# Another order of the calls on TensorE, ScalarE and VectorE in the recurrent part of a gated delta-rule kernel

## The reference, cut to what matters

```python
mixed = silu(conv4(xn @ W_qkv))            # 4 taps per channel, over time
q, k, v = split(mixed)                     # 16 key heads, each used by 2 value heads
q, k = l2norm(q) * DK ** -0.5, l2norm(k)
def step(S, xs):                           # token by token, S is 128 x 128 for a head
    S = S * exp(g_t)
    S = S + beta_t * k_t[:, None] * (v_t - k_t @ S)[None, :]
    return S, q_t @ S
o = o * rsqrt(mean(o * o) + 1e-6) * norm_w * silu(xn @ W_z)
s = o @ W_out
```

## Time and profile before

| what | value |
|---|---|
| median of 3 runs | 2795.55 us (2793.66 to 2805.6) |
| the profiled execution's own time | 2802.01 us |
| its span in the profile | 2800.1 us |
| TensorE busy | 2619.4 us, 94% |
| DVE, ScalarE, GpSimd busy | 71%, 58%, 38% |
| mean granted TensorE clock | 0.985 |

### The profile page before, as it was taken

How to read it: one execution, slowest core, us unless ns; L and a number is a source line. 1 busy time by engine, 2 the same in 40 slices (tenths; PEclk the granted TensorE clock), 3 DMA queues, 4 the chain that set the end, 5 groups by cost and what they waited for, 6 DMA issues and landing times.

```text
span 2800.1 us, 87430 instructions
## 1 busy us (share of the span) xinstructions
PE 2619.4 (94%) x34330; PEld 1946.0 (69%) x34330; DVE 2001.6 (71%) x4880; ACT 1610.8 (58%) x5046; POOL 1075.5 (38%) x1391
## 2 busy tenths in 40 slices
PE   2999997999999999999999999999999999999995
PEld 2456655777777777777777777777777777777774
DVE  5322235888878887888778877887778878888773
ACT  2111114666666666666666666666666666666662
POOL 0312203444444444444444444444444444444440
PEclk8999998999999999999999999999999999999997
DMA  4322301111111111111111111111111111111112
GB/s 148 76 53 64 64 1 53 46 54 46 53 46 54 46 54 46 54 46 54 46 53 46 54 46 53 47 43 49 43 49 50 49 49 50 50 50 50 50 50 64
DMA packets 225654, 146.99 MB, mean 52 GB/s; under 512 B 187456, under 2 KB 195936, under 8 KB 225120
## 3 DMA queue, kind: packets, MB, share of 16 engines
q1 hardware_dynamic: 219104, 123.58, 15.5%
q0 software_dynamic: 6144, 17.83, 2.8%
HBM read 115.81 MB, written 2.70 MB: 42 GB/s over the span
## 4 chain that ended last, share of the span: by engine, by line
PE 66%; DVE 8%; ACT 3%; issue 2%; DMA 2%; SPq 1%; POOL 1%; DVEq 0%; POOLq 0%; ACTq 0%
PE rps L809 12%; PE rps L734 8%; PE rps L742 8%; DVE conv L1262 6%; PE rps L696 4%; PE rps L826 4%; PE rps L713 4%; PE rps L865 3%; PE rps L856 3%; PE rps L839 3%; PE rps L680 3%; PE rps L706 3%; PE rps L774 3%; PE rps L783 3%; PE rps L683 2%
## 5 line engine op out<-in xcount | busy, mean ns | idle before, releaser
L1262 DVE SCALAR_TENSOR_TENSOR conv<-rps,w_in,conv 128x509 f32<-128x509 f32 (+2 forms) x768 | 572.0, 745 | 64.6 <-ACT conv L1050 46.4
L809 PE MATMUL rps<-xnT,w_in 128*128 128x512 f32 x1024 | 504.3, 615 | 13.9 <-DVE cols L1244 13.0
L1461 POOL TENSOR_TENSOR decay_b<-decay,beta_k 128x512 f32<-128x512 f32 x128 | 130.6, 1042 | 487.6 <-DVE beta_k L1278 487.6
L1412 POOL TENSOR_TENSOR o_t<-o_sq,q_mean 128x8 f32<-128x8 f32 x65 | 13.4, 206 | 691.0 <-ACT gated L983 691.0
L809 PEld LDWEIGHTS rps<-xnT,w_in 128*128 128x128 f32 x1024 | 174.8, 190 | 148.2 <-issue 125.2
L742 PE MATMUL rps<-w_z,xnT 128*128 128x256 f32 x1040 | 275.1, 387 | 1.0 <-ACT z L999 0.7
L1050 ACT ACTIVATE conv<-rps,w_in 128x512 f32<-128x512 f32 x256 | 176.1, 688 | 164.5 <-PE rps L809 161.5
L734 PE MATMUL rps<-w_outn,gatedT 128*128 128x256 f32 x1056 | 241.3, 381 | 1.0 <-ACT gatedT L993 0.7
L734 PEld LDWEIGHTS rps<-w_outn,gatedT 128*128 128x128 f32 x1056 | 201.6, 191 | 49.7 <-issue 23.8
L1064 ACT ACTIVATE qkT<-conv 128x512 f32<-128x512 f32 x128 | 80.5, 629 | 222.1 <-DVE conv L1262 222.1
L742 PEld LDWEIGHTS rps<-w_z,xnT 128*128 128x128 f32 x1040 | 183.1, 191 | 21.6 <-ACT z L999 1.1
(11 more groups left out here) (217 smaller groups left out, 6477.4 us busy)
## 6 DMA issues: line engine op xcount, KB each, us to landing
sums_row<-g_rows SPq DMA_DIRECT2D x65, 1024.0 KB, 5.0
scale<-comb_rows POOLq DMA_DIRECT2D x40, 256.0 KB, 5.0
w_in<-in_w_in SPq DMA_DIRECT2D x17, 520.0 KB, 3.5
bq<-bmat SPq DMA_DIRECT2D x256, 32.0 KB, 2.0
inv<-xq SPq DMA_DIRECT2D x256, 32.0 KB, 1.9
w_z<-in_w_z SPq DMA_DIRECT2D x17, 256.0 KB, 2.6
w_out<-in_w_out SPq DMA_DIRECT2D x17, 256.0 KB, 5.0
invT<-xqT SPq DMA_DIRECT2D x128, 32.0 KB, 2.2
```

What stands on the lines that cost most here:

```text
L809: last = nc.tensor.matmul(ps[PROJ_BANK[j]][:, :], w_in[:, m * 4 * P + j * P:m * 4 * P + (j + 1) * P], xnT[:, m, b * T:(b + 1) * T], start= ...
L1262: nc.vector.scalar_tensor_tensor(conv[:, j, shift:T], ps[PROJ_BANK[j]][:, 0:T - shift], w_in[:, k:k + 1], conv[:, j, shift:T], ALU.mult, A ...
L1461: nc.gpsimd.tensor_tensor(decay_b[:, us, :], decay[:, us, :], beta_k2[:, us].unsqueeze(2).to_broadcast([P, NC_, C]), ALU.mult).then_inc(db ...
```

## The change

The same calls stand in another order in the lists of TensorE, ScalarE and DVE, inside the loop over steps. GpSimd's and SyncE's lists are as before. No call is added or dropped, and the waits inside a call go with it.

```diff
@@ TensorE
                     project(0)
+                    halves_w(n)
                     by_token(1)
-                    halves_w(n)
                     project(2)
...
                     solve(0)
                     project(3)
-                    attend(0)
                     pe.wait_ge(tap_done, n(12) + 6)
                     gated_transpose(n, 1)
+                    attend(0)
+                    by_token(0)
                     read_state(1)
-                    by_token(0)
+                    k_products(0)
                     solve(1)
-                    by_token(2)
-                    k_products(0)
+                    pe.wait_ge(ksq_done, n(1) + 1)
+                    pe.wait_ge(kw_done, n(2) + 2)
+                    project_out(n, 0, loads)
+                    project_out(n, 1, loads)
                     attend(1)
                     pe.wait_ge(wz_in, (i + (1 if b == 0 else 2)) * 16)
                     pe.wait_ge(tap_done, n(12) + 12)
                     project_z(tb, 0)
                     read_state(2)
+                    spread_rows()
                     project_z(tb, 1)
+                    by_token(2)
                     solve(2)
-                    spread_rows()
-                    pe.wait_ge(ksq_done, n(1) + 1)
-                    pe.wait_ge(kw_done, n(2) + 2)
-                    project_out(n, 0, loads)
-                    project_out(n, 1, loads)
                     pe.wait_ge(qsq_done, n(1) + 1)
                     project_out(n, 2, loads)
                     project_out(n, 3, loads)
@@ ScalarE
                     first_tap(0)
+                    take_halves(n)
                     squares_by_token(1)
-                    take_halves(n)
                     silu(0)
                     first_tap(2)
+                    take_updates(0)
+                    take_transposes(n, 0)
+                    silu(2)
                     if b == 2:
                         act.wait_ge(out_ps, n(2))
                         scale_out_weights(i + 2)
-                    take_updates(0)
                     first_tap(3)
-                    take_transposes(n, 0)
                     take_transposes(n, 1)
-                    silu(2)
+                    squares_by_token(0)
                     take_state_part(1)
                     take_updates(1)
                     exp_decay((b + 1) % BATCH, n(4) + 8, n(2) + 2, 0)
-                    squares_by_token(0)
                     exp_decay((b + 1) % BATCH, n(4) + 8, n(2) + 2, 1)
+                    gate_z(n, 0)
                     take_state_part(2)
-                    squares(0)
                     take_updates(2)
                     silu(3)
                     take_v(0)
+                    squares(0)
                     take_merge(0)
...
                     take_merge(1)
-                    gate_z(n, 0)
+                    take_v(1)
                     gate_z(n, 1)
-                    take_v(1)
@@ DVE
                     new_state(0)
                     output(0)
+                    decayed_k(0)
                     residual(1)
+                    decayed_k(1)
                     taps(3)
+                    compact()
                     new_state(1)
                     output(1)
-                    compact()
-                    decayed_k(0)
+                    scores_of_head(0)
                     residual(2)
-                    decayed_k(1)
                     substitute()
                     new_state(2)
                     output(2)
-                    scores_of_head(0)
+                    add_out(n, (b - 2) % BATCH, 0)
                     residual(3)
-                    add_out(n, (b - 2) % BATCH, 0)
                     scores_of_head(1)
                     merge(0)
+                    add_out(n, (b - 2) % BATCH, 1)
                     output(3)
-                    add_out(n, (b - 2) % BATCH, 1)
                     merge(1)
```

## The result

The changed kernel takes 2795.63 us (median of 20 runs, 2790.87 to 2799.26), the kernel before 2801.0 us in as many runs beside them (2793.66 to 2805.6). The ratio is 0.9981, with a 95% interval of 0.9974 to 0.9987: 0.19% less, about 5.4 us, where I had forecast 10.9 us. It lies in my range and within the 0.5% that held most of the chance, but the size is half of the forecast. The profiled execution has a span of 2791.6 us, 8.5 less than before.

What follows compares the result with a forecast made beforehand. TensorE's queue and its stops were taken as the bound; places of 0.05, 0.12 and 0 us gave 0.17 a step, 10.9 us over 64 steps, so 2785 us from 2795.55, range 2769 to 2803.

Steps and rivals of the forecast that it cites:

- First place: halves_w ahead of by_token(1): gain 0.05 us a step, from +0.33 with all copies on time to -0.41 with all late.
- Second place: by_token(0) and k_products(0) ahead of solve(1), whose 0.10 us wait goes: gain 0.12 us a step, bounds 0 and 0.16.
- Third place: compact() ahead of new_state(1), read_state(2) and spread_rows ahead of solve(2): slack stays 0.8 us, cost 0.
- The step that failed: gate_z(0) ahead of take_updates(2) on ScalarE: over some 1.5 us after project_z(1)'s end, about 0.9 of cover left, no cost.
- The pauses of merge_x: Unexplained stops in merge_x's 32x32 matmuls on TensorE, 0.4 us a step: about as before, a third either way being 9 us.
- The rival "nothing": More late copies eat the gain, or instruction-placed merge pauses shift 9 us either way: 2796 us, chance 0.22.
- My sign of a slower kernel: In the new profile, read_state(2) or attend(2) on TensorE waiting in every step would mean slower than predicted.
- The full gain: Copies for halves_w land in time in nearly all steps: 0.45 us a step, 29 us, 2767 us, chance 0.15.
- the slower case by compact: compact waits for bq copies, new_state(1) and output(1) behind it on DVE: 0.4 us a step lost, 2821 us, chance 0.11.

Runs made afterwards that it cites:

- f1_split: The changed kernel with halves_w waiting only for the first two copies, which it reads, and halves_x for all four: 2770.95 us, ratio 0.9891 to before.
- e2_early_load: The changed kernel with a one-column silu, which waits for nothing, added ahead of gate_z(0) on ScalarE: 2767.44 us, ratio 0.9888 to before.
- e4_halves_alone: The kernel before with only halves_w moved ahead of by_token(1) and take_halves ahead of squares_by_token(1): 2788.73 us, ratio 0.9968 to before.
- e3_halves_back: The changed kernel with by_token(1) again ahead of halves_w and squares_by_token(1) ahead of take_halves: 2793.09 us, ratio 0.9982 to before.

## Why the prediction was half right

I cut each step at three calls of the time line (start of join_w, end of halves_x, taken as the start of the call behind it, and start of merge_w) and averaged the pieces over the same 61 steps of each kernel, in us:

| piece | before | after | gain | forecast |
|---|---|---|---|---|
| step start to halves_x | 8.56 | 8.55 | 0.01 | 0.05 |
| to merge_w | 17.36 | 17.58 | -0.22 | 0.12 |
| to the step's end | 9.75 | 9.38 | 0.37 | 0 |
| whole step | 35.67 | 35.51 | 0.16 | 0.17 |

The profiled pair thus gains 10 us by these steps and 8.5 us in the span, the medians 5.4. The total in these traces is near the forecast, but by terms that cancel: terms of 0.35, 0.15 and -0.47 that I all had at 0. That the time fell into the range is luck.

*First place.* Right in the main. The shortest head of a step fell from 8.50 to 8.17, the 0.33 of my sum; TensorE comes to halves_w at offset 3.72 (forecast 3.71); the late landings cost 17.9 us over 51 steps, 0.35 each, within the 15 to 25 us expected. I misread one row: the 18 idle places of the earlier trace rows are 8 of matmuls (2.6 us) and 10 of the weight loads of the same calls (4.7 us), not 18 steps. The landings in the trace before give 48% of the steps on time, 36% between and 16% late, where I had set 40, 35 and 25. The section of the Trainium skill that I named ("DMA: Bandwidth & Descriptors", the anatomy of one DMA) gives its 2.0 us for a DMA issued by GpSimd, and these are issued by SyncE; here the time from issue to landing was no constant but 1.9 to 4.1 us. What I did not ask is whether halves_w needs the copies that are late. It doesn't (f1_split).

*Second place.* Right: 0.10 in the shortest middle (17.18 before, 17.08 in e2_early_load), and solve(1) at 0.61.

*Third place.* Mis-sized. I set it at 0, since I argued the slack ahead of the masks would stay. By the shortest middles, late events cost 0.18 a step before (17.36 less 17.18) and 0.03 after (17.58 less 17.55), a gain of 0.15. compact sat behind GpSimd for 3.9 us in 10 places, not for 10.2 in 14, and read_state(2) has no row among the first waits, where I expected 14 steps. The landing of the masks' copies had a maximum of 3.1 us in the changed kernel's trace; whether they are less late by the order or by the execution is not settled.

*The step that failed*: "The rest costs nothing by its cover", in which gate_z(0) "is over some 1.5 us later with the state part and the update". It costs 0.47 us a step (shortest middle 17.55 against 17.08 in e2_early_load), 30 us, or 26 us by the ratios: the load of 1.28 us stands behind gate_z's wait. The 0.9 of cover that I counted less the load of 1.28 is -0.38, and 0.36 is how late attend(2) starts. The kernel before held the fact in one row, a load of L1064 in each step; I looked at what the moved calls take and not at what ScalarE switches between them.

*The pauses of merge_x.* I had them unchanged, and put a third more or less of them, 9 us, into the range. They lost 0.35 us a step (merge_x(0) and (1) together last 1.93 before and 1.58 after), 22 us. In the waits from 600 to 2400 us the three kernels with the old middle have 15.1 to 21.9 us of them. Those with the new middle of TensorE as it stands have 4.0 to 7.4 us where the load still stops TensorE (at attend(2) or merge_x), and 6.6 to 10.5 without that stop. So the new order in the middle thins them, and the stop can have only a small part in it. Which of its moves does it stays open.

Where they stand can be read from the traces. Number the recorded instructions of TensorE's queue (weight loads, matmuls and its waits) in order of time, from 0. A step has 1054 of them. In all thirteen traces together merge_x has 288 pauses over 0.15 us, and each of them stands at number 193 or 194 above a multiple of 256. The order of calls doesn't move these places, since the counts are the same: number 21186, in a merge_x, has a pause before and after the change.

```profile
1088.22 0.28 PE L865 MATMUL rps<-xq,wq 32*32 32x32 f32 x9 [1.11 <-issue]
1088.82 0.28 PE L865 MATMUL rps<-xq,wq 32*32 32x32 f32 x9 [0.60 <-issue]
```

So the pauses do follow the place of instructions in TensorE's stream, as my rival said. Something happens every 256 instructions of the queue that can hold it up (before 1.11 us, after 0.60 in these rows), and the order of the other calls changes how long it does. What it is, and why the new middle makes it shorter, no run here shows.

Summed: 0.01, 0.10, 0.15 and 0.35 less 0.47 are 0.14, where the direct difference is 0.16. The rival "nothing" had the merge pauses at 9 us either way; they gave 22. My sign of a slower kernel, attend(2) waiting in every step, came, and the pauses paid for it. The full gain and the slower case by compact did not come.

## What to carry to other kernels

When a call moves on ScalarE, list for each activation which table it needs, and see which call becomes the first user after a switch: if that one waits for another engine, its load, 1.28 us here, is added behind the wait. Give the load to a call whose input is ready, or to a one-column activation. When a wait on DMAs shows up, compare what the semaphore counts with what the instruction reads, before moving the instruction: here that split gave 24 us on e4_halves_alone and 25 us on the changed kernel, against 5 us for the whole change.

## What the runs showed of the hardware

- A table load (1283 ns in the mean, in every kernel) at the first activation after a switch started only when the semaphores of this activation had come, even after 1.86 us of idle (L999 in the changed kernel).
- Of four small SBUF copies of 32 KB, issued in the same pattern in each step, the third and fourth land 1.9 us after issue in the median but up to 4.1 us. A wait that stood right behind the median was hit in 14 to 23 places in 51 steps (e4_halves_alone and the changed kernel).
- The 32x32 matmuls of merge_x pause for up to 1.4 us without a releaser. Their total over 51 steps is 21.9 us in the kernel before and 4.0 in e3_halves_back, between which only the order of calls differs. All 288 such pauses of the thirteen traces stand a multiple of 256 recorded instructions of TensorE's queue apart, give or take one.
